# Four moves at the head of each batch of a state-space layer: dt's transfers, early scalings, MLP products, the lag of the sums

## The chip, the cores and the metric

The kernel runs on one core of a Trainium2 chip. The metric is the device time of one execution, in microseconds (us), lower being better. TensorE (PE in the rows) multiplies, PEld is its weight load, VectorE is DVE, ScalarE is ACT, GpSimd is POOL and SyncE, which issues the transfers, is SP.

## The reference, cut to what matters

Four layers run over x of 8 batches x 512 steps x 256 columns. Three are attention layers that the change doesn't touch. The fourth is a state-space layer with an MLP behind it. Its core, once forward and once on the flipped sequence, with 512 inner channels and 32 states:

```python
xdbl = x @ x_proj_W
dt = softplus(xdbl[..., :DT_RANK] @ dt_proj_W + dt_proj_b)
Bm = xdbl[..., DT_RANK:DT_RANK + D_STATE]
Cm = xdbl[..., DT_RANK + D_STATE:]
A = -exp(A_log)
def step(hst, inp):
    dt_t, B_t, C_t, x_t = inp
    dA = exp(dt_t[:, :, None] * A)
    hst = hst * dA + dt_t[:, :, None] * B_t[:, None, :] * x_t[:, :, None]
    y = einsum('bdn,bn->bd', hst, C_t)
    return (hst, y)
...
x = x + g1[:, None, :] * (fwd + bwd)
h = _ln(x, norm2_w, norm2_b)
h = h * (1.0 + s2[:, None, :]) + sh2[:, None, :]
mlp = silu(h @ w1) * (h @ w2) @ w3
return x + g2[:, None, :] * mlp
```

## The kernel before

The last layer (`mamba_layer`, L1770) takes the batches one after another. A batch is cut into 128 **units**: the forward direction is units 0 to 63, the backward one 64 to 127, and unit i handles chunk i % 4 of the channels with group i // 4 of two states (`NJ`). 128 partitions hold 64 channels x 2 states, and two such halves stand in a row of 1024. Per unit:

- ScalarE makes two decays exp(dt A) from `dt_rep` (`decay_unit`, L1957).
- dt B x: per group of four units, eight scalings (`OPS`) of `dtx_T` by a column of B give `dtx_B`. They are numbered 0 to 7. `pool_ops(k)` says how many of the last ones GpSimd makes for group k (`scale_last`, L1941); for group 0 VectorE makes the first `VEC_OPS` (`scale_first`, L1950); ScalarE makes the rest (`scale_pair`, L1933), six units ahead.
- TensorE transposes `dtx_B` into PSUM (`fill_bx`, L1967), eight transposes, called a fill here. Fill i+1 waits for scan i-1.
- VectorE scans (L2546): h = decay h + dtx_B over 1024 elements. Scan i needs fill i, its decays, and the product of unit i-3, since `h` has three slots.
- GpSimd multiplies h by C (L2512, "product with C"), into one of seven slots `hc_of`. Four of them are a tensor `hc` of their own, which lies where `dt_all` lay, three lie in slots of x.
- TensorE sums that over the states (`y_sum`, L2634), some units behind: `BEHIND` units, one fewer for each eight units from `CATCH_UP` on, never under two. Batch 0 keeps two throughout.

Between two batches come the gates, the convolution, projections and softplus of the next batch. `between_sync` sends dt out into `dt_rep`: a transfer for each of four chunks, two halves and two states, 16 in all, each with both directions (L1981). After them `sync_batch` sends C, row pair by row pair for each group (`c_rep`, four slots, L2472). At group 3 it waits for GpSimd's two additions of the MLP's result (`mlp_add`, L2505), stores the batch before, loads a new x, and only then sends C for that group.

The MLP of batch b-1 runs beside the first scans of batch b. `tanh_up` on ScalarE (L2283), a pair of products on VectorE (`mlp_products`, L2191 and L2194), three times in all (j = 0, 1, 2); the up-projections (`up_half`, L2390) and the down-projection (`down`, L2395) on TensorE, by unit in `mlp_step`; the residual (L2562) on VectorE, twice; the additions on GpSimd at units 8 and 9. The order on each engine is written out by hand: `if i in (1, 3)` puts a pair of products behind scans 1 and 3. The first fill's waits are in `first_fill`.

The first batch (0) is prepared while the layer before is running, and a barrier of all engines stands between its preparation and its first scan.

## Time and profile before

| | |
|---|---|
| median of 3 runs | 5861.52 us (5860.26 to 5861.61) |
| the profiled execution | 5858.16 us, span 5856.3 us, granted TensorE clock 0.986 |
| last layer's scans | from 3112.7 to the end of the span, 8 batches of some 346 us |
| busy over the span | PE 94%, DVE 75%, ACT 69%, POOL 48% |

The span is the time from the first to the last instruction of the profiled execution. Starts in the rows are us from the span's start. "Idle before" is the time that the engine stood before an instruction, and behind the arrow is what ended it. The granted clock is a share of TensorE's full 2.4 GHz; 0.5 is 1.2 GHz.

### The profile page before, as it was taken

How to read it: one execution, taken by the hardware profiler on the slowest of the kernel's cores; microseconds unless marked ns; L12 is line 12 of the kernel's file. 1: busy time of each engine (PE TensorE's matmuls, PEld its weight loads, DVE VectorE, ACT ScalarE, POOL GpSimd, SP SyncE). 2: the span in 40 equal slices, each digit the busy share in tenths (PEclk: the TensorE clock that was granted, in tenths of full speed). 3: DMA queues.
4: the chain of work that ended last, by engine and by line, in shares of the span. 5: the costliest groups of instructions: out<-in, count | busy, mean ns of one | idle time of the engine just before them, and what ended most of it. 6: DMA issues, size and time to landing. Idle time of an engine off the chain costs nothing. (4 is left out here: it accounts for less than half of the span.)

```text
span 5856.3 us, 74768 instructions
## 1 busy us (share of the span) xinstructions
PE 5526.3 (94%) x27336; PEld 2880.5 (49%) x27336; DVE 4380.6 (75%) x5135; ACT 4059.9 (69%) x6684; POOL 2809.0 (48%) x2191
## 2 busy tenths in 40 slices
PE   8999999999999997999998999999998999999998
PEld 5444445555555554444444444454544444454545
DVE  6767744444444445776768989999998999989998
ACT  3555454454445553555548979899898989979897
POOL 0000012232222320010107969699696979959697
PEclk8999999999999998999999999999999999999999
DMA  5242410000000004233223020110212111020110
GB/s 145 47 66 33 87 26 2 1 3 3 2 3 1 3 8 58 55 59 70 51 48 75 30 57 30 46 40 24 63 31 55 32 36 51 26 61 30 46 37 22
DMA packets 173663, 228.63 MB, mean 39 GB/s; under 512 B 41073, under 2 KB 107466, under 8 KB 173042
## 3 DMA queue, kind: packets, MB, share of 16 engines
q1 hardware_dynamic: 173298, 223.85, 17.4%
q8 instruction: 218, 3.57, 0.3%
q14 instruction: 147, 1.20, 0.1%
HBM read 156.05 MB, written 33.64 MB: 32 GB/s over the span
## 5 line engine op out<-in xcount | busy, mean ns | idle before, releaser
L2546 DVE TENSOR_TENSOR_SCAN l__h<-l__decay,psum 128x1024 f32<-128x1024 f32 x1024 | 2253.5, 2268 | 81.9 <-PE psum L1967 30.8
L1957 ACT ACTIVATE l__decay<-l__dt_rep,l__a_neg 128x511 f32<-128x511 f32 x2048 | 1342.9, 709 | 84.1 <-DVE l__h L2546 46.8
L1967 PEld LDWEIGHTS psum<-ident,l__dtx_B 128*128 128x128 f32 x8192 | 892.2, 142 | 938.0 <-DVE l__h L2546 578.4
L1967 PE MATMUL psum<-ident,l__dtx_B 128*128 128x128 f32 x8192 | 1126.1, 281 | 116.3 <-DVE l__h L2546 51.3
L2512 POOL TENSOR_TENSOR l__hc<-l__h,l__c_rep 128x1024 f32<-128x1024 f32 x584 | 1170.3, 2039 | 96.5 <-DMA l__c_rep<-l__c_dram 90.8
L1933 ACT ACTIVATE l__dtx_B<-l__dtx_T,l__b_T 128x512 f32<-128x512 f32 x1624 | 1079.5, 710 | 28.8 <-PE psum L1967 22.6
L2512 POOL TENSOR_TENSOR x_sb<-l__h,l__c_rep 128x1024 f32<-128x1024 f32 x432 | 867.1, 2040 | 32.4 <-DVE l__h L2546 20.4
L684 DVE TENSOR_REDUCE l__row_max<-psum 128x1 f32<-128x512 f32 x1024 | 648.6, 680 | 206.0 <-PE psum L718 202.3
L1373 POOL TENSOR_SCALAR l__probs<-l__probs,l__rec 128x512 f32<-128x512 f32 x512 | 349.8, 698 | 888.3 <-DVE l__rec L1369 888.3
L200 POOL TENSOR_SCALAR l__ln_var_eps<-l__ln_mean_var 128x4 f32<-128x4 f32 x56 | 16.1, 288 | 1428.5 <-DVE l__ln_mean_var L186 1428.5
L2634 PE MATMUL psum<-l__hc,l__gather 128*64 128x512 f32 x2368 | 637.2, 618 | 36.9 <-POOL l__hc L2512 36.2
L1046 ACT ACTIVATE l__probs<-psum 128x1024 f32<-128x1024 f32 x512 | 502.1, 1024 | 145.9 <-PE psum L1107 139.5
L1359 DVE TENSOR_REDUCE l__neg_max<-psum 128x2 f32<-128x1024 f32 x256 | 301.8, 1218 | 319.6 <-PE psum L1353 319.6
L2634 PE MATMUL psum<-x_sb,l__gather 128*64 128x512 f32 x1728 | 464.1, 617 | 27.4 <-POOL x_sb L2512 27.2
L1534 ACT ACTIVATE l__probs_T<-psum 128x512 f32<-128x512 f32 x256 | 152.3, 595 | 402.8 <-PE psum L1584 401.4
L718 PE MATMUL psum<-l__k_stack,l__q_stack 96*128 96x512 bf16 (+1 forms) x1024 | 380.1, 392 | 28.5 <-DVE l__row_max L684 13.9
L1941 POOL TENSOR_SCALAR l__dtx_B<-l__dtx_T,l__b_T 128x512 f32<-128x512 f32 x384 | 280.1, 729 | 155.3 <-ACT l__dtx_T L2243 154.6
L1364 ACT ACTIVATE l__probs<-psum,l__neg_max 128x512 f32<-128x512 f32 x512 | 347.3, 690 | 6.2 <-DVE l__neg_max L1359 6.1
L1107 PE MATMUL psum<-l__q_stack,l__k_stack 98*128 98x512 bf16 (+1 forms) x1024 | 302.8, 385 | 23.4 <-DMA l__q_stack<-l__max_rows 16.1
L1584 PEld LDWEIGHTS psum<-ident,l__probs 128*128 128x128 f32 x2048 | 227.6, 141 | 167.1 <-issue 98.5
L1584 PE MATMUL psum<-ident,l__probs 128*128 128x128 f32 x2048 | 278.5, 278 | 9.7 <-DVE l__probs_T L1481 7.3
L1120 PE MATMUL psum<-l__probs,l__v_and_ones 128*32 128x512 f32 x2048 | 274.3, 608 | 9.6 <-ACT l__probs L1046 9.6
(190 smaller groups left out, 6727.9 us busy)
## 6 DMA issues: line engine op xcount, KB each, us to landing
l__c_rep<-l__c_dram SPq DMA_DIRECT2D x512, 128.0 KB, 2.8
l__dt_rep<-l__dt SPq DMA_DIRECT2D x128, 256.0 KB, 5.0
l__parts_dram<-l__parts SPq DMA_DIRECT2D x64, 384.0 KB, 3.4
l__q_stack<-l__parts_dram SPq DMA_DIRECT2D x192, 128.0 KB, 6.6
l__k_stack<-l__parts_dram SPq DMA_DIRECT2D x192, 128.0 KB, 9.4
l__w<-in_l_w SPq DMA_DIRECT2D x6, 1024.0 KB, 7.6
l__gate_rows<-l__gates_dram SPq DMA_DIRECT2D x24, 256.0 KB, 3.3
in_mod_w<-in_mod_w SPq DMA_DIRECT2D x1, 4608.0 KB, 17.6
```

What stands on the lines that cost most here:

```text
L684: nc.vector.tensor_reduce(mx[:, n // GT, n % GT:n % GT + 1], max_bank(n), AX.X, ALU.max).then_inc(S["max_taken"], 1)
L718: nc.tensor.matmul(max_bank(n), qs[0:k_max, h, t * P:(t + 1) * P], ks[0:k_max, h, :], start=True, stop=True).then_inc(S["max_filled"], 1)
L1046: nc.scalar.activation(probs[:, n % SLOTS:n % SLOTS + 2, :], pair(n), ACT.Exp, scale=float(HD) ** -0.5).then_inc(S["exp"], 1)
L1364: nc.scalar.activation(probs[:, u % SLOTS, j, :], bank[QK + 2 * (u % 2) + j], ACT.Exp, bias=neg_max[:, u % SLOTS, j:j + 1], accum_out=sums ...
L1373: nc.gpsimd.tensor_scalar(probs[:, u % SLOTS, j, :], probs[:, u % SLOTS, j, :], rec[:, u % SLOTS, j:j + 1], 1.0, ALU.mult, ALU.mult)\
L1584: last = nc.tensor.transpose(bank[TR + j][:, k * P:(k + 1) * P], probs[:, u % SLOTS, j, k * P:(k + 1) * P], ident[:, :])
L1933: nc.scalar.activation(dtx_B[:, (k + 1) % 2, t, :, j, :], dtx_T[:, w, t, :].rearrange("p (b d) -> p b d", d=HB), ACT.Copy, scale=b_T[:, w, ...
L1957: nc.scalar.activation(decay[:, i % DECAYS, s, 1:T], dt_rep[:, w, c, s, 1:T], ACT.Exp, scale=a_neg[:, g, c, s:s + 1]).then_inc(S["decay"], 1)
L1967: last = nc.tensor.transpose(bx_psum(i)[:, s, t * P:(t + 1) * P], dtx_B[:, (k + 1) % 2, t, 2 * c + s, :, :].rearrange("p j d -> p (j d)"), ...
L2512: nc.gpsimd.tensor_tensor(hc_of(i), h[:, i % HS, :, :], c_of(i), ALU.mult).then_inc(S["hc"], 1)
L2546: nc.vector.tensor_tensor_scan(both(h[:, i % HS, :, :]), both(decay[:, i % DECAYS, :, :]), both(bx_psum(i)), 0.0, ALU.mult, ALU.add).then_ ...
L2634: last = nc.tensor.matmul(y_psum[half(s), c, :], gather[:, :], row, start=(w == 0 and g == 0), stop=(w == 1 and g == GROUPS - 1))
```

## The change

- `between_sync` sends the forward half of dt alone, 16 transfers of 128 KB. A new `back_sync` sends the backward half in 16 more, behind C's transfers for group 0. GpSimd waits for all of dt at unit 3, not at unit 0; ScalarE waits for the backward half at unit 64.
- The order of the seven slots is turned: the first three products go into slots of x, which dt's transfers don't read, and the wait for spilled batches moves with them from unit 4 to unit 0 of batch 0.
- Scalings: VectorE makes three of group 0 and not five, ScalarE three and not two, GpSimd two and not one. Of group 1 GpSimd makes four and not two, and all before the scans. In a batch GpSimd has 51 and not 48, 45 and not 47 of them between its products.
- The MLP's pairs of products stand behind scans 0, 1 and 4, not before scan 0 and behind 1 and 3. `tanh_up(0)` goes behind group 0's scalings and decay 1. The three down-projection steps go one unit later each. The first residual stands behind scan 6, not 5.
- `CATCH_UP` is 80, not 40.

```diff
-    pool_ops = lambda k: 1 + k % 2
-    VEC_OPS = 5
+    pool_ops = lambda k: {0: 2, 1: 4}.get(k, 1 + k % 2)
+    VEC_OPS = 3
...
-    RESIDUAL_AFTER, ADD_AT, STORE_AT, ROWS_FIRST_AT = (5, 7), (8, 9), 3, 10
-    BEHIND, CATCH_UP = 7, 40
+    PRODUCTS_AFTER, RESIDUAL_AFTER, ADD_AT, STORE_AT, ROWS_FIRST_AT = (0, 1, 4), (6, 7), (8, 9), 3, 10
+    BEHIND, CATCH_UP = 7, 80
...
-            if n < HCS - 3:
-                return hc_first[:, n, :, :]
-            return x[:, KEPT + n - (HCS - 3), :, :].rearrange("p (s u) d -> p s (u d)", s=2)
+            if n >= 3:
+                return hc_rest[:, n - 3, :, :]
+            return x[:, KEPT + n, :, :].rearrange("p (s u) d -> p s (u d)", s=2)
...
-                        sp.dma_start(dt_rep[half(j), :, c, s, :], dt_all[half(s), c, :, :]).then_inc(s_dt_rep[c], 16)
+                        sp.dma_start(dt_rep[half(j), 0, c, s, :], dt_all[half(s), c, 0, :]).then_inc(s_dt_rep[c], 16)
             sp.wait_ge(*S.at("c_out", 32))
+
+        def back_sync(sp):
+            for c in range(IC):
+                for s in range(2):
+                    for j in range(NJ):
+                        sp.dma_start(dt_rep[half(j), 1, c, s, :], dt_all[half(s), c, 1, :]).then_inc(s_dt_back, 16)
...
-                scale_last(0, range(NJ - pool_ops(0), NJ))
+                scale_last(0, range(OPS - pool_ops(0), OPS))
+                scale_last(1, range(OPS - pool_ops(1), OPS))
...
             scale_first(dve)
-            if end:
-                mlp_products(dve, 0, 0)
...
             first_decay(act, 0, nxt)
             take_forward(2)
             take_forward(3)
-            if end:
-                tanh_up(act, 0, 0)
...
             for i in range(1, DECAYED):
                 first_decay(act, i, nxt)
+            if end:
+                tanh_up(act, 0, 0)
...
+                if k == 0:
+                    back_sync(sp)
...
-                if i == 0:
+                if i == 3:
                     for c in range(IC):
                         pool.wait_ge(s_dt_rep[c], dt_rep_of(b))
+                    pool.wait_ge(s_dt_back, dt_back_of(b))
...
-                if i in (1, 3) and S.batch:
-                    mlp_products(dve, (i + 1) // 2, HC)
+                if i in PRODUCTS_AFTER and S.batch:
+                    mlp_products(dve, PRODUCTS_AFTER.index(i), HC)
```

The order of VectorE's instructions at the start of batch 1, before. `l__h` is the scan, `l__dtx_B` the early scalings, `x_sb<-x_sb,psum` the MLP's products, `x_sb<-psum,l__gate_rows` a residual:

```order
L1950 TENSOR_SCALAR l__dtx_B<-l__dtx_T,l__b_T 128x8x64 x5
L2191 SCALAR_TENSOR_TENSOR x_sb<-x_sb,psum 128x512
L2194 SCALAR_TENSOR_TENSOR x_sb<-x_sb,psum 128x512
L2546 SCALAR_TENSOR_TENSOR l__h<-l__decay,psum 128x1024 x2
L2191 SCALAR_TENSOR_TENSOR x_sb<-x_sb,psum 128x512
L2194 SCALAR_TENSOR_TENSOR x_sb<-x_sb,psum 128x512
L2546 SCALAR_TENSOR_TENSOR l__h<-l__decay,psum 128x1024 x2
L2191 SCALAR_TENSOR_TENSOR x_sb<-x_sb,psum 128x512
L2194 SCALAR_TENSOR_TENSOR x_sb<-x_sb,psum 128x512
L2546 SCALAR_TENSOR_TENSOR l__h<-l__decay,psum 128x1024 x2
L2562 TENSOR_TENSOR x_sb<-psum,l__gate_rows 128x512
```

The same place on VectorE with the change:

```order
L1953 TENSOR_SCALAR l__dtx_B<-l__dtx_T,l__b_T 128x8x64 x3
L2556 SCALAR_TENSOR_TENSOR l__h<-l__decay,psum 128x1024
L2199 SCALAR_TENSOR_TENSOR x_sb<-x_sb,psum 128x512
L2202 SCALAR_TENSOR_TENSOR x_sb<-x_sb,psum 128x512
L2556 SCALAR_TENSOR_TENSOR l__h<-l__decay,psum 128x1024
L2199 SCALAR_TENSOR_TENSOR x_sb<-x_sb,psum 128x512
L2202 SCALAR_TENSOR_TENSOR x_sb<-x_sb,psum 128x512
L2556 SCALAR_TENSOR_TENSOR l__h<-l__decay,psum 128x1024 x3
L2199 SCALAR_TENSOR_TENSOR x_sb<-x_sb,psum 128x512
L2202 SCALAR_TENSOR_TENSOR x_sb<-x_sb,psum 128x512
L2556 SCALAR_TENSOR_TENSOR l__h<-l__decay,psum 128x1024 x2
L2571 TENSOR_TENSOR x_sb<-psum,l__gate_rows 128x512
```

Two scalings are gone, scan 0 stands ahead of the first products, and three scans stand between the second and the third pair.

The order on GpSimd from the last preparation of batch 1 on, before (`l__dtx_B` is a scaling, `l__h,l__c_rep` a product with C, into `hc` or a slot of x):

```order
L2104 MEMSET l__decay 128x6
L1941 TENSOR_SCALAR l__dtx_B<-l__dtx_T,l__b_T 128x8x64
L2512 TENSOR_TENSOR l__hc<-l__h,l__c_rep 128x1024
L1941 TENSOR_SCALAR l__dtx_B<-l__dtx_T,l__b_T 128x8x64
L2512 TENSOR_TENSOR l__hc<-l__h,l__c_rep 128x1024
L1941 TENSOR_SCALAR l__dtx_B<-l__dtx_T,l__b_T 128x8x64
L2512 TENSOR_TENSOR l__hc<-l__h,l__c_rep 128x1024 x2
```

The same place with the change:

```order
L2113 MEMSET l__decay 128x6
L1944 TENSOR_SCALAR l__dtx_B<-l__dtx_T,l__b_T 128x8x64 x6
L2522 TENSOR_TENSOR x_sb<-l__h,l__c_rep 128x1024 x3
L2522 TENSOR_TENSOR l__hc<-l__h,l__c_rep 128x1024
L1944 TENSOR_SCALAR l__dtx_B<-l__dtx_T,l__b_T 128x8x64
```

Six scalings come ahead of the first product, and none stands between the first four.

The order of SyncE's transfers from batch 0 to batch 1, before:

```order
L1976 DMA l__c_dram<-l__dt_and_c 32x512 x2
L1981 DMA l__dt_rep<-l__dt 64x2x512 x16
L2472 DMA l__c_rep<-l__c_dram 64x512 x6
L2833 DMA out_x<-x_sb 128x4x256
```

And with the change:

```order
L1979 DMA l__c_dram<-l__dt_and_c 32x512 x2
L1984 DMA l__dt_rep<-l__dt 64x512 x16
L2480 DMA l__c_rep<-l__c_dram 64x512 x2
L1991 DMA l__dt_rep<-l__dt 64x512 x16
L2480 DMA l__c_rep<-l__c_dram 64x512 x4
L2844 DMA out_x<-x_sb 128x4x256
```

C's first pair now stands behind 16 transfers of half the size, and 16 more stand ahead of its second pair.

## Rows read from the trace of the kernel before

**Rows 1.** Groups of the page: op, out<-in, count | busy us, mean ns | idle before

```profile
L2546 DVE TENSOR_TENSOR_SCAN l__h<-l__decay,psum 128x1024 f32<-128x1024 f32 x1024 | 2253.5, 2268 | 81.9 <-PE psum L1967 30.8
...
L2512 POOL TENSOR_TENSOR l__hc<-l__h,l__c_rep 128x1024 f32<-128x1024 f32 x584 | 1170.3, 2039 | 96.5 <-DMA l__c_rep<-l__c_dram 90.8
```

**Rows 2.** GpSimd's busy time by stretch of batch 1: stretch, us, busy (count), clock

```profile
3446.90:3482.30 35.40, 23.73 (x16) 0.90 0.25 61
...
3500.00:3745.70 245.70, 244.80 (x157) 1.00 0.08 28
```

**Rows 3.** The chain of waits, start of batch 1: start, us, what

```profile
3450.49 4.24 DMA l__c_rep<-l__c_dram
...
3454.80 2.00 POOL l__hc L2512
...
3460.21 1.94 PE psum L1967 x8
3462.16 3.41 PE psum L2395 x8
...
3466.66 2.16 PE psum L2395 x10
```

**Rows 4.** Timeline of GpSimd, batch 1, and in the last row batch 7

```profile
3474.34 2.01 POOL L2512 TENSOR_TENSOR l__hc<-l__h,l__c_rep 128x1024 f32<-128x1024 f32 x1 [0.24 <-PE psum L2634]
...
3482.34 3.96 POOL L2512 TENSOR_TENSOR l__hc<-l__h,l__c_rep 128x1024 f32<-128x1024 f32 x2
...
3491.08 3.96 POOL L2512 TENSOR_TENSOR x_sb<-l__h,l__c_rep 128x1024 f32<-128x1024 f32 x2 [2.15 <-DMA l__c_rep<-l__c_dram]
...
5560.92 3.96 POOL L2512 TENSOR_TENSOR l__hc<-l__h,l__c_rep 128x1024 f32<-128x1024 f32 x2
```

**Rows 5.** Timeline of VectorE, batch 1, and in the last row batch 7

```profile
3446.89 4.46 DVE L2546 TENSOR_TENSOR_SCAN l__h<-l__decay,psum 128x1024 f32<-128x1024 f32 x2
...
3453.19 0.69 DVE L2194 SCALAR_TENSOR_TENSOR x_sb<-x_sb,psum 128x512 f32<-128x512 f32 x1
...
3468.90 0.67 DVE L2562 TENSOR_TENSOR x_sb<-psum,l__gate_rows 128x512 f32<-128x512 f32 x1
...
3474.69 2.28 DVE L2546 TENSOR_TENSOR_SCAN l__h<-l__decay,psum 128x1024 f32<-128x1024 f32 x1
...
5525.26 4.46 DVE L2546 TENSOR_TENSOR_SCAN l__h<-l__decay,psum 128x1024 f32<-128x1024 f32 x2
```

**Rows 6.** Timeline of the sync queue's transfers into batch 1: start, us of issuing, count

```profile
3433.43 15.73 SPq L1981 DMA_DIRECT2D l__dt_rep<-l__dt  x16
3449.26 9.89 SPq L2472 DMA_DIRECT2D l__c_rep<-l__c_dram  x6
```

**Rows 7.** All engines by stretch: us, PE, PEld, DVE, ACT, POOL, clock, DMA, GB/s

```profile
3440.00:3450.00 10.00, 8.69 (x43) 5.14 (x42) 7.97 (x11) 8.39 (x14) 0.70 (x1) 1.00 1.06 237
...
3454.00:3459.00 5.00, 0.63 (x2) 0.00 (x0) 4.14 (x2) 5.00 (x9) 4.20 (x3) 1.00 0.15 52
3459.00:3466.00 7.00, 5.79 (x20) 4.99 (x21) 3.77 (x4) 5.56 (x10) 7.00 (x6) 0.51 0.11 40
```

**Rows 8.** Timeline of ScalarE, batch 1

```profile
3453.91 2.56 ACT L1957 ACTIVATE l__decay<-l__dt_rep,l__a_neg 128x511 f32<-128x511 f32 x4 [1.48 <-DMA l__dt_rep<-l__dt]
```

**Rows 9.** Who writes `dtx_B`, ns min/median/max: VectorE in batch 1, GpSimd in batch 3

```profile
L1950 DVE TENSOR_SCALAR l__dtx_B<-l__dtx_T,l__b_T x5: 467/473/789, 3443.1 to 3445.0; 128x512 f32<-128x512 f32 x5
...
L1941 POOL TENSOR_SCALAR l__dtx_B<-l__dtx_T,l__b_T x1: 994/994/994, 4137.2 to 4137.2; 128x512 f32<-128x512 f32 x1
```

**Rows 10.** Timeline of TensorE, batches 1 and 3

```profile
3495.56 1.09 PE L1967 MATMUL psum<-ident,l__dtx_B 128*128 128x128 f32 x8 [2.22 <-DVE l__h L2546]
...
4137.06 2.58 PE L2390 MATMUL psum<-x_sb,l__w 128*128 128x512 f32 x4 [1.93 <-ACT l__dtx_T L2243]
...
4145.18 1.88 PE L2390 MATMUL psum<-x_sb,l__w 128*128 128x512 f32 x4
```

**Rows 11.** Timeline of GpSimd, batch 0

```profile
3127.22 3.98 POOL L2512 TENSOR_TENSOR x_sb<-l__h,l__c_rep 128x1024 f32<-128x1024 f32 x2
```

More of the change, by code:

```diff
@@ L1787, in mamba_layer @@
     ADDED_AT = tuple(range(4 * IC, 8 * IC, IC))
-    pool_ops = lambda k: 1 + k % 2
-    VEC_OPS = 5
-    scaled = lambda groups: sum(OPS - pool_ops(k % GROUPS) for k in range(1, groups + 1)) \
+    pool_ops = lambda k: {0: 2, 1: 4}.get(k, 1 + k % 2)
+    VEC_OPS = 3
+    scaled = lambda groups: sum(OPS - pool_ops(k % (2 * GROUPS)) for k in range(1, groups + 1)) \
         - (VEC_OPS if groups == UNITS // IC else 0)
-    pool_scaled = lambda groups: sum(pool_ops(k % GROUPS) for k in range(1, groups + 1))
-    RESIDUAL_AFTER, ADD_AT, STORE_AT, ROWS_FIRST_AT = (5, 7), (8, 9), 3, 10
-    BEHIND, CATCH_UP = 7, 40
+    pool_scaled = lambda groups: sum(pool_ops(k) for k in range(2, min(groups + 1, 2 * GROUPS))) \
+        + (pool_ops(0) + pool_ops(1) if groups == UNITS // IC else 0)
+    PRODUCTS_AFTER, RESIDUAL_AFTER, ADD_AT, STORE_AT, ROWS_FIRST_AT = (0, 1, 4), (6, 7), (8, 9), 3, 10
+    BEHIND, CATCH_UP = 7, 80
     FILLED = 2
@@ L1852, in mamba_layer @@
         dt_rep_of = lambda b: PER_CHUNK * (b + 1)
+        s_dt_back = nc.alloc_semaphore(f"{tag}_dt_back")
+        dt_back_of = lambda b: PER_CHUNK * IC * (b + 1)
         psum = consts["psum"]
@@ L1928, in scale_pair @@
             w, g, _ = split(k * IC)
-            for op in (2 * c, 2 * c + 1)[0:NJ - pool_ops(k) if c == IC - 1 else NJ]:
-                if k == 0 and op < VEC_OPS:
+            for op in (2 * c, 2 * c + 1):
+                if op >= OPS - pool_ops(k) or k == 0 and op < VEC_OPS:
                     continue
@@ L1938, in scale_last @@
             w, g, _ = split(k * IC)
-            t = TT - 1
-            for j in ops:
+            for op in ops:
+                t, j = op // NJ, op % NJ
                 nc.gpsimd.tensor_scalar(dtx_B[:, (k + 1) % 2, t, :, j, :],
@@ L2346, in first_fill @@
                 pe.wait_ge(*S.at("dtxB", scaled(UNITS // IC) if end else OPS - pool_ops(0) - VEC_OPS))
-                pe.wait_ge(*S.at("dtxB_pool", pool_scaled(UNITS // IC) if end else pool_ops(0)))
+                pe.wait_ge(*S.at("dtxB_pool", pool_scaled(UNITS // IC) - pool_ops(1) if end else pool_ops(0)))
                 pe.wait_ge(*S.at("dtxB_vec", VEC_OPS))
@@ L2408, in mlp_step @@
                         down(pe, t, j)
-            if i == 4:
+            if i == 5:
                 pe.wait_ge(*S.at("prod", 0))
@@ L2415, in mlp_step @@
                 down(pe, 2, 2)
-            if i == 5:
+            if i == 6:
                 for j in range(HC):
@@ L2489, in gpsimd_batch @@
                 k = i // IC + 1
-                if i % IC == (1 if k == 1 else 0) and k < UNITS // IC:
-                    if k >= 2:
-                        pool.wait_ge(*S.at("bx_filled", IC * (k - 1) - FILLED))
-                    scale_last(k, (NJ - pool_ops(k),))
-                if i % IC == (2 if k == 1 else 1) and k < UNITS // IC and pool_ops(k) == 2:
-                    scale_last(k, (NJ - 1,))
+                if i % IC == 0 and 2 <= k < UNITS // IC:
+                    pool.wait_ge(*S.at("bx_filled", IC * (k - 1) - FILLED))
+                    scale_last(k, (OPS - pool_ops(k),))
+                if i % IC == 1 and 2 <= k < UNITS // IC and pool_ops(k) == 2:
+                    scale_last(k, (OPS - 1,))
                 if i % IC == 0:
                     pool.wait_ge(*S.at("c_rep", 16 * NJ * (i // IC + 1)))
-                if i == 0:
+                if i == 3:
                     for c in range(IC):
                         pool.wait_ge(s_dt_rep[c], dt_rep_of(b))
+                    pool.wait_ge(s_dt_back, dt_back_of(b))
                 if i in ADD_AT and S.batch:
@@ L2506, in gpsimd_batch @@
                     pool.wait_ge(*S.at("mlp_add", k - 1))
-                if i == HCS - 3 and b == 0:
+                if i == 0 and b == 0:
                     pool.wait_ge(s_spill, 16 * (B - KEPT))
@@ L2593, in decays @@
                     act.wait_ge(s_dt_rep[i], dt_rep_of(b))
+                if i == UNITS // 2:
+                    act.wait_ge(s_dt_back, dt_back_of(b))
                 decay_unit(i)
@@ L2598, in scalar_batch @@
             for i in range(UNITS):
-                if i in (1, 3) and S.batch:
-                    tanh_up(act, (i + 1) // 2, HC)
+                if i in PRODUCTS_AFTER[1:] and S.batch:
+                    tanh_up(act, PRODUCTS_AFTER.index(i), HC)
                 if i + DECAYED < UNITS:
```

5 lines of the change are left out of this document (2 added, 3 removed).

## The prediction

> **What bounds the kernel now.** The change touches the last layer alone, so I read in this order: the costliest groups, GpSimd's time by stretch, the chain of waits at the start of a batch, and the timelines of GpSimd and VectorE there.
>
> In the groups the reader should see two operations of nearly the same size per unit: the scan on VectorE and the product with C on GpSimd, both some 2.0 to 2.3 us [rows 1]. GpSimd also has 1.5 scalings for every 4 units. In batch 1 GpSimd is busy 244.8 us of the 245.7 us from unit 16 or so to unit 126, so it sets the pace there; in the 35.4 us before, it works 23.7 us [rows 2]. What can be won lies in those first 35 us, and a gain there is kept only if it reaches GpSimd.
>
> The chain of waits says what fills them [rows 3]. It comes down the sync queue's sixteen dt transfers, through C's first transfer (lands 3454.7), the first product with C (3454.8), a scaling behind it, and then TensorE at half clock: 8 transposes in 1.94 us, 8 matmuls of the MLP in 3.41 us. That first product starts 7.9 us after scan 0, and the tenth, unit 9, at 3482.34 [rows 4], 35.45 us after scan 0 [rows 5]. In the last batch, 7, that distance is 35.66 us, and over the seven batches with an MLP beside the scans, read from the same rows of each, it is 34.9 in the mean [rows 4, 5]. I use it as the yardstick, and call the start of scan 0 time 0.
>
> **The transfers.** Before, sixteen dt transfers of 256 KB take the sync queue 15.73 us, and C's follow at 3449.26, or +2.4 [rows 6]. The DMA engines are full at 237 GB/s meanwhile [rows 7], so 256 KB need 1.1 us and the issue time (0.98 us) is their backlog. Sixteen of 128 KB should take 0.6 us each: they begin at -13.5 as before and end at -3.9. C's first pair goes out by -2.6 and, with the 4.24 us of [rows 3], lands by +1.6, ahead of scan 0's end at +2.2. The sixteen backward ones follow from -2.6 to +7 and land by about +10; C's second pair lands by +11.5. Unit 3's product, which now waits for all dt, cannot begin before +11.7, and unit 4's, which needs C's second pair, not before +14.4. So they cost nothing, with 1.7 us to spare at the tighter place. ScalarE's waits for dt, the longest 1.48 us [rows 8], go.
>
> **The first fill.** VectorE's five early scalings take 2.4 us (last start 3445.0, first 3443.1, and 0.47); the first took 0.79 us instead of 0.47 beside GpSimd's one, and where VectorE began first GpSimd's took 0.99, 0.3 us over its usual time [rows 9]. They get in each other's way by about 0.3 us. Now VectorE has three and GpSimd runs six beside them: three of 0.41 us plus three meetings of 0.3 to 0.4 us make 2.2 to 2.4 us. Bounds: with no further meeting the fill comes 0.43 us sooner, which is how long TensorE idled before it; if every one costs a whole slot, 0.2 us later. I take 0, because the meeting is in the rows. The Trainium skill (SBUF — State Buffer, "SBUF: two separate sides") says that the port pair shared by VectorE's two-port mode and GpSimd is an exclusive lock for a whole instruction, which speaks against giving GpSimd more scalings here. By that rule the seven starts lose 1.4 us together; without it they gain 3.0 us; the traces fit the lock. ScalarE has three scalings (2.0 us) and GpSimd's first two are done in time. Its four for the second group end at about +0.5, under the wait for scan 0. No such scaling is left between the first products, so TensorE's fill 4 no longer waits for one.
>
> **VectorE from scan 0 to scan 8.** A scan takes a 2.2 us slot, a pair of MLP products 1.4, a residual 0.7 [rows 5]. In the new order: scan 0 ends 2.2, products 3.6, scan 1 5.8, products 7.2, scans 2 to 4 13.9, products 15.3, scans 5 and 6 19.7, residual 20.4, scan 7 22.6, residual 23.2, where scan 8 starts. It is 8 x 2.2 + 3 x 1.4 + 2 x 0.7 = 23.2 us of plain work; before, batch 1 took 27.8 us although one pair was done ahead of scan 0 [rows 5]. Who must be ready:
> - ScalarE: three scalings, decay 1, tanh 0 by -0.1, four scalings 2.4, decay 2 3.7, tanh 1 4.3 (needed 5.8). Ready.
> - TensorE at full clock, a fill 1.09 and an up-projection 1.88 us [rows 10]: fill 2 ends 3.8 (needed 7.2), fill 3 7.0 (9.4), fill 4 10.6 (11.7), fill 5 12.8 (15.3), eight down matmuls at 0.22 us each (from ten in 2.16 us [rows 3]) 14.7, fill 6 15.8 (17.5), ten more 18.1, fill 7 19.2 (20.4). Ready each time.
> - GpSimd: products 0 to 3 start at 2.3, 5.9, 9.5, 11.7; scan 5 needs product 2, ended 11.5, and scan 6 product 3, ended 13.7. Ready.
>
> **The sum.** Product 7 starts after scan 7 and the first sum, at 22.9. From there to product 9 GpSimd has the same work as before, 3474.34 to 3482.34, 8.0 us [rows 4]. Product 9 thus starts at 30.9 against 34.9: 4.05 us won, seven times, 28.4 us. From there on nothing changes: the wait of 2.15 us before unit 12 [rows 4] is for C's fourth pair, behind the store that GpSimd's second addition releases, and it moves along.
>
> Batch 0 has no MLP and starts behind a barrier that waits for the queue's issues. Product 4 starts at 3127.22 [rows 11]. The barrier opens about 1 us sooner, but now product 3 waits for the backward dt (some 3123) and C's second pair comes after it (some 3125.5): I take 1.1 us won, bounds 0 and 3.
>
> The longer lag of the sums (7 up to unit 80) costs nothing: units up to 40 have had it, and GpSimd still idles under 1 us in 245 [rows 2]. Without that cover each product would wait for its slot as unit 7 does, 0.24 us [rows 4].
>
> Sum: 28.4 + 0 + 1.1 = 29.5 us. The profiled execution took 5858.2 us, so 5828.7 in its terms. The median of the runs is 3.4 us above it, 5861.5, and my forecast is on that: 5832 us, 0.50% less.
>
> **The rivals.**
> - *TensorE falls to half clock again.* It does so soon after pauses of 1.93 and 2.22 us [rows 10]; my order leaves it 0.7 and 1.1 us near +9 to +12, shorter, but close together. At half clock the eight down matmuls take 3.4 instead of 1.75 us and a fill 1.94, which makes scan 7 late by 1.3 to 2.1 us: 9 to 15 us over seven batches, 5841 to 5847. Against it: the 5 us with 0.63 us of TensorE work that came before a granted clock of 0.51 in 3459 to 3466 [rows 7] are gone. Chance 0.16.
> - *Slower: a transfer costs the queue the same whatever its size.* If 128 KB take 1.0 us each as 256 KB do, C's first pair lands at +7.9 as before, the backward sixteen are issued until +20 and land by +25. Product 3 begins then instead of at +15.2, product 4 at +27.7, product 9 at about +41.5: 6.6 us lost seven times, and some 10 in batch 0, 5918. For it: C's own first 128 KB took 1.19 us. Against: that was behind the backlog, and six C transfers together span 9.89 us with their landings waited for in between [rows 6]. It starts to cost when a backward transfer takes over 0.9 us (14.3 us from -2.6 to +11.7, by sixteen). Chance 0.05.
> - *The gain is swallowed at unit 12.* If C's fourth pair came at a fixed time and not 8.7 us after GpSimd's additions, six of the seven gains would end in that wait: 5857. The queue's store follows the addition at once in batch 1, so little speaks for it. Chance 0.05.
>
> **Numbers.** My forecast has 0.74, in a range of its own from 5822 to 5840 (no meeting on the port -3, batch 0 -2, a batch's late half-clock stretch behind unit 12 up to 1 us in four batches, and up to 1 us a batch that my hand-made order has missed). This kernel's measurement can tell some 0.2%, 12 us, from no change. The range for 8 in 10 takes in the clock case: 5818 to 5850. Faster by over 0.2% (below 5849.8): 0.74 and nearly all of 0.16, 0.88. Within 0.2%: 0.07. Slower: 0.05.
>
> **What would show it.** Right: product 0 within 0.2 us of scan 0's end in batches 1 to 7; scan 8 at 23 to 24 us after scan 0; product 9 at about 31; granted clock 1.00 in the first 20 us; no wait for dt on ScalarE or GpSimd; three VectorE scalings that take 2.2 us or more together, and scan 0 within 0.3 us of where it was behind the scan before it. Wrong: TensorE rows of 0.45 us there (first rival), product 3 or 4 released by a transfer in batches 1 to 7 (second), a wait before unit 12 of 6 us in place of 2 (third). If scan 8 comes at 23 and product 9 later than 32, GpSimd's path has something that I have not seen.

## The result and the profile after

The changed kernel took **5822.99 us** (median of 4 runs, 5820.22 to 5827.71) against 5860.89 (5858.82 to 5861.61) for the kernel before on the same chip: ratio 0.9937, 95% interval 0.9921 to 0.9952. A second set on another chip gave 5824.93 us and 0.994 [0.9926, 0.9953]. The forecast was 5832 us, in 5818 to 5850. The profiled executions, which I compare below, took 5820.22 us (span 5818.4, granted clock 0.989) after and 5858.16 before, 37.9 us apart, where the sum said 29.5.

The groups, in the same columns as [rows 1], show the same two operations at nearly the same size. The first three products of a batch now stand in slots of x, so both of GpSimd's groups have to be read: together they idled 128.9 us before, 102.8 of them for C's transfers, and idle 77.5 now, 21.0 of them for C. The largest releaser is now the scan.

```profile
L2556 DVE TENSOR_TENSOR_SCAN l__h<-l__decay,psum 128x1024 f32<-128x1024 f32 x1024 | 2252.3, 2267 | 60.9 <-POOL l__hc L2522 20.6
...
L2522 POOL TENSOR_TENSOR l__hc<-l__h,l__c_rep 128x1024 f32<-128x1024 f32 x576 | 1145.1, 2010 | 27.0 <-DVE l__h L2556 13.2
...
L2522 POOL TENSOR_TENSOR x_sb<-l__h,l__c_rep 128x1024 f32<-128x1024 f32 x440 | 876.1, 2010 | 50.5 <-DVE l__h L2556 40.1
```

The sync queue's timeline into batch 1 answers to [rows 6]. Sixteen transfers of 128 KB take 10.10 us to issue, C's first pair goes at 3442.36, and the backward sixteen take as long again. The second-last row is the store of the previous batch, the last C behind it.

```profile
3432.17 10.10 SPq L1984 DMA_DIRECT2D l__dt_rep<-l__dt  x16
3442.36 1.18 SPq L2480 DMA_DIRECT2D l__c_rep<-l__c_dram  x2
3443.58 10.37 SPq L1991 DMA_DIRECT2D l__dt_rep<-l__dt  x16
3454.00 5.32 SPq L2480 DMA_DIRECT2D l__c_rep<-l__c_dram  x4
3475.80 0.41 SPq L2844 DMA_DIRECT2D out_x<-x_sb  x1
...
3479.76 15.79 SPq L2480 DMA_DIRECT2D l__c_rep<-l__c_dram  x10
```

VectorE's timeline of batch 1 answers to [rows 5]. Scan 0 starts at 3445.60, scan 8 at 3468.18, 22.58 us later, with no idle time in between. Behind the three early scalings (2.35 us) it idles 1.41 us for the first fill.

```profile
3441.85 2.35 DVE L1953 TENSOR_SCALAR l__dtx_B<-l__dtx_T,l__b_T 128x512 f32<-128x512 f32 x3
3445.60 2.29 DVE L2556 TENSOR_TENSOR_SCAN l__h<-l__decay,psum 128x1024 f32<-128x1024 f32 x1 [1.41 <-issue]
3447.80 0.66 DVE L2199 SCALAR_TENSOR_TENSOR x_sb<-x_sb,psum 128x512 f32<-128x512 f32 x1
...
3449.10 2.28 DVE L2556 TENSOR_TENSOR_SCAN l__h<-l__decay,psum 128x1024 f32<-128x1024 f32 x1
...
3467.60 0.67 DVE L2571 TENSOR_TENSOR x_sb<-psum,l__gate_rows 128x512 f32<-128x512 f32 x1
3468.18 4.45 DVE L2556 TENSOR_TENSOR_SCAN l__h<-l__decay,psum 128x1024 f32<-128x1024 f32 x2
```

GpSimd's timeline of the same stretch answers to [rows 4]. Each of the first products waits for its scan, not for a transfer. Product 9 starts at 3475.80, 30.20 us after scan 0. The wait before unit 12 is still there, 1.95 us against 2.15.

```profile
3441.56 4.52 POOL L1944 TENSOR_SCALAR l__dtx_B<-l__dtx_T,l__b_T 128x512 f32<-128x512 f32 x6 [15.04 <-ACT l__dtx_T L2251]
3448.04 2.00 POOL L2522 TENSOR_TENSOR x_sb<-l__h,l__c_rep 128x1024 f32<-128x1024 f32 x1 [1.96 <-DVE l__h L2556]
3451.46 2.00 POOL L2522 TENSOR_TENSOR x_sb<-l__h,l__c_rep 128x1024 f32<-128x1024 f32 x1 [1.42 <-DVE l__h L2556]
...
3467.83 2.00 POOL L2522 TENSOR_TENSOR x_sb<-l__h,l__c_rep 128x1024 f32<-128x1024 f32 x1 [0.84 <-DVE l__h L2556]
...
3475.80 2.00 POOL L2522 TENSOR_TENSOR x_sb<-l__h,l__c_rep 128x1024 f32<-128x1024 f32 x1
...
3484.34 3.96 POOL L2522 TENSOR_TENSOR l__hc<-l__h,l__c_rep 128x1024 f32<-128x1024 f32 x2 [1.95 <-DMA l__c_rep<-l__c_dram]
```

All engines by stretch, in the columns of [rows 7]: the hole of 5 us in which TensorE worked 0.63 us is a stretch with 3.20 us of work, and the granted clock behind it is 1.00 where it was 0.51.

```profile
3454.00:3459.00 5.00, 3.20 (x22) 2.65 (x22) 5.00 (x3) 4.09 (x7) 3.78 (x2) 1.00 0.47 108
3459.00:3466.00 7.00, 7.00 (x45) 5.99 (x43) 6.96 (x7) 6.47 (x12) 5.87 (x5) 1.00 0.10 37
```

Read from the start rows of scans and products in each batch, means of batches 1 to 7 in us:

| | before | after | difference, seven batches |
|---|---|---|---|
| last scan of a batch to scan 0 | 49.89 | 49.49 | 2.8 |
| scan 0 to product 0 | 7.89 | 2.44 | |
| scan 0 to scan 8 | 27.28 | 22.58 | |
| scan 0 to product 9 | 34.92 | 30.21 | 33.0 |
| product 9 to the last scan | 260.97 | 260.86 | 0.8 |

That is 36.6 us. Batch 0 gave nothing, and the layer's first softplus came 1.3 us sooner (3092.67 against 3094.00): 37.9. I take the last as chance and not as an effect of the change: in the profiles of this study that softplus starts anywhere from 3092.7 to 3102.7 us (3097.95 in a second profile of the changed kernel, e12), though no edit here touches what runs ahead of it. So I judge an edit by its distances inside the batches first and by the ratio second.

### The profile page after: what moved, and what is told of

The parts are those of the page before. It is cut to its first block and busy times, and to the rows that moved or that the text cites. A ratio compares the mean times of both kernels' runs of the same rounds, so it can differ in the third digit from the quotient of the medians.

```text
span 5818.4 us, 74898 instructions
## 1 busy us (share of the span) xinstructions
PE 5519.2 (95%) x27336; PEld 2866.2 (49%) x27336; DVE 4375.3 (75%) x5119; ACT 4054.8 (70%) x6676; POOL 2826.3 (49%) x2215
## 5 line engine op out<-in xcount | busy, mean ns | idle before, releaser
L2522 POOL TENSOR_TENSOR l__hc<-l__h,l__c_rep 128x1024 f32<-128x1024 f32 x576 | 1145.1, 2010 | 27.0 <-DVE l__h L2556 13.2
L2645 PE MATMUL psum<-l__hc,l__gather 128*64 128x512 f32 x2304 | 618.3, 618 | 12.0 <-POOL l__hc L2522 12.0
L2645 PE MATMUL psum<-x_sb,l__gather 128*64 128x512 f32 x1792 | 483.2, 619 | 12.8 <-POOL x_sb L2522 12.3
```

What stands on the lines that cost most here:

```text
L2522: nc.gpsimd.tensor_tensor(hc_of(i), h[:, i % HS, :, :], c_of(i), ALU.mult).then_inc(S["hc"], 1)
L2645: last = nc.tensor.matmul(y_psum[half(s), c, :], gather[:, :], row, start=(w == 0 and g == 0), stop=(w == 1 and g == GROUPS - 1))
```

## The experiments

Each starts from the changed kernel. They ask which of the four moves brought the 33 us, why it was more than the sum said, and whether the costs I saw (the meeting of VectorE's and GpSimd's scalings, unit 12) are what I took them for. Where two medians of different experiments are compared, their ratios to the kernel before on the same chip say more than the microseconds.

### e1: dt sent whole again

```diff
-    sp.dma_start(dt_rep[half(j), 0, c, s, :], dt_all[half(s), c, 0, :]).then_inc(s_dt_rep[c], 16)
+    sp.dma_start(dt_rep[half(j), :, c, s, :], dt_all[half(s), c, :, :]).then_inc(s_dt_rep[c], 16)
...
-    if k == 0:
-        back_sync(sp)
```

(The two waits for the backward half go as well.)

> The changed kernel, but with dt's forward and backward halves sent together again in sixteen transfers, ahead of C's. C's first pair then lands at about +7.9 us after scan 0, as before the change, not at +2.4. My theory: with no scaling between the first products and VectorE's work spread out, that costs little. Product 0 at 7.9, product 1 at 9.9, scan 3 starts at 9.9 in place of 9.2, scan 4 at 12.1; product 9 at 31 to 31.5 us and not 30.2. 0.8 to 1.3 us a batch, 6 to 9 us over seven, and 2.4 us more if one batch's decay 0 waits for dt as batch 3's did: 5829 to 5834 us. Rival: C's first transfer is on the path all the way, as the chain of waits of the kernel before has it. Then the 5.5 us by which it lands later show in full at product 9, seven times: some 5860 us.

Measured: 5833.97 us (5831.4 to 5837.19), ratio 0.9956 [0.9941, 0.9971], at the upper end of what was expected. Product 0 at 8.0, scan 8 at 23.96, product 9 at 32.26 us, 0.8 later than expected. The sixteen transfers take 15.87 us again. TensorE's timeline of batch 1 shows the half clock that the prediction had as a rival: a pause of 1.80 us, a fill in 1.97 us instead of 1.06, eight down matmuls in 2.63 instead of 1.89. The down matmuls then push the first sum to 3468.65, and the last row, GpSimd's, shows product 7 waiting for it.

```profile
3455.39 1.06 PE L1970 MATMUL psum<-ident,l__dtx_B 128*128 128x128 f32 x8 [0.78 <-DVE l__h L2553]
3458.26 1.97 PE L1970 MATMUL psum<-ident,l__dtx_B 128*128 128x128 f32 x8 [1.80 <-DVE l__h L2553]
3460.02 2.63 PE L2403 MATMUL psum<-l__w,x_sb 128*128 128x256 f32 x8
...
3468.65 1.08 PE L2640 MATMUL psum<-x_sb,l__gather 128*64 128x512 f32 x4
```

```profile
3469.82 2.00 POOL L2519 TENSOR_TENSOR x_sb<-l__h,l__c_rep 128x1024 f32<-128x1024 f32 x1 [1.61 <-PE psum L2640]
```

The split is worth 2.05 us a batch up to product 9 and 0.33 between batches, over half of the latter in batch 3 (1.26 of 2.3). That is 16.7 of the 36.6 us, not all of it: something else in the change must bring the rest even with C late.

### e2: the scalings in their old places

```diff
-    pool_ops = lambda k: {0: 2, 1: 4}.get(k, 1 + k % 2)
-    VEC_OPS = 3
+    pool_ops = lambda k: 1 + k % 2
+    VEC_OPS = 5
...
-                scale_last(1, range(OPS - pool_ops(1), OPS))
```

> The changed kernel with the scalings as before: five on VectorE, one on GpSimd ahead of the scans, two of group 1 between the first products. My theory: with C landing early, GpSimd has 1.42 and 1.49 us idle ahead of products 1 and 2, which take in the two scalings of 0.66 us; the last one ends by +8.5, fill 4 starts at +11.1. VectorE's five alone take what three took beside six of GpSimd's (2.36 and 2.35 us). So product 9 stays at 30.2 us, gap between batches as it is, 5823 us within 4. Rival: the two scalings more in GpSimd's stretch cost their 1.3 us a batch, product 9 at 31.5, 5832 us.

Measured: 5821.61 us (5816.07 to 5832.45), ratio 0.9931 [0.9915, 0.9948]; product 9 at 30.22 and the gap before scan 0 49.43 us, against 30.21 and 49.49. With C early the moved scalings are worth nothing, because GpSimd idles before each of its first three products anyway (1.96, 1.42 and 1.49 us in batch 1 of the changed kernel): in e2 its two scalings of group 1 are done 8.54 us after scan 0, and fill 4, which needs them, starts at 9.43 in both kernels.

### e3: the MLP's products in their old places

```diff
-    PRODUCTS_AFTER, RESIDUAL_AFTER, ADD_AT, STORE_AT, ROWS_FIRST_AT = (0, 1, 4), (6, 7), (8, 9), 3, 10
+    PRODUCTS_AFTER, RESIDUAL_AFTER, ADD_AT, STORE_AT, ROWS_FIRST_AT = (0, 1, 3), (5, 7), (8, 9), 3, 10
...
             scale_first(dve)
+            if end:
+                mlp_products(dve, 0, 0)
...
-                if i in PRODUCTS_AFTER and S.batch:
+                if i in PRODUCTS_AFTER[1:] and S.batch:
```

(tanh 0 goes back ahead of ScalarE's scalings, and each group of down matmuls goes one unit earlier, as before.)

> The changed kernel with the MLP's order as before: first pair of products and tanh 0 ahead of scan 0, pairs behind scans 1 and 3, down steps and first residual one unit earlier. My theory: in the changed kernel VectorE idles 1.41 us ahead of scan 0, so the first pair is free there and costs 1.3 us behind scan 0. Undone, with dt and C early enough, VectorE's plain work from scan 0 to scan 8 falls from 22.6 to 21.2 us and all that it waits for is ready: product 9 at 29 us, 1.0 to 1.3 us a batch faster, 5814 to 5816 us. Rival: the move was what took ScalarE's tanh and TensorE's down steps off the path (1.1 us wait for tanh, 1.7 to 2.2 us before scans 4 and 5 in the kernel before), so that undoing it gives back 1 to 3 us a batch: 5830 to 5844 us.

Measured: 5814.48 us (5810.77 to 5817.78), ratio 0.9922 [0.9907, 0.9937], the gap unchanged at 49.49 us, scan 8 at 21.27 and product 9 at 28.88. **The MLP move costs 1.33 us a batch, 9.3 in all.** VectorE idles 1.41 us for the first fill; a pair of products takes 1.3 us and fits in there, as its timeline in this kernel shows:

```profile
3443.41 2.34 DVE L1953 TENSOR_SCALAR l__dtx_B<-l__dtx_T,l__b_T 128x512 f32<-128x512 f32 x3
3445.67 0.67 DVE L2201 SCALAR_TENSOR_TENSOR x_sb<-x_sb,psum 128x512 f32<-128x512 f32 x1
3446.37 0.69 DVE L2204 SCALAR_TENSOR_TENSOR x_sb<-x_sb,psum 128x512 f32<-128x512 f32 x1
3447.16 4.46 DVE L2558 TENSOR_TENSOR_SCAN l__h<-l__decay,psum 128x1024 f32<-128x1024 f32 x2
```

The change takes the pair out of that hole and puts it behind scan 0, where VectorE is the bound: here it is busy 28.81 of the 28.88 us from scan 0 to product 9 (stretch, us, busy and count, clock, share and rate of the DMA).

```profile
3447.16:3476.04 28.88, 28.81 (x18) 1.00 0.36 87
```

### e4: the longer lag of the sums alone undone

```diff
-    BEHIND, CATCH_UP = 7, 80
+    BEHIND, CATCH_UP = 7, 40
```

> The changed kernel with CATCH_UP 40 in place of 80. My theory: GpSimd sets the pace from unit 16 on and the sums wait for nobody: the same time within 2 us, and from unit 40 to 80 the same distance. Rival: sums that run closer behind the products make TensorE wait for GpSimd and delay its fills: up to 0.24 us a unit in units 40 to 80, which would be over 5 us a batch.

Measured: 5823.94 us (5820.12 to 5830.79), ratio 0.994 [0.9925, 0.9955]. Units 40 to 80 take 90.29 us, and 90.31 with the longer lag. It does nothing.

### e8 and e10: one move alone, and two without the split

e8 keeps the split and undoes scalings and MLP order, the diffs of e2 and e3 together.

> The changed kernel with both the scalings and the MLP's order as before: of the change only the split of dt, the turned slots and the lag are left. My theory: what the two undone parts were worth each by itself (nothing, and a loss of 1.32 us a batch) adds up, as GpSimd has idle time for the scalings there too: product 9 at 28.9 us, 5814 us within 4. Rival: with VectorE 1.3 us further ahead, the scalings between the first products now hold up fill 4 or GpSimd: product 9 at 29.5 to 30.2, 5819 to 5823 us.

Measured: 5819.48 us (5815.93 to 5821.0), ratio 0.9923 [0.9909, 0.9936]; product 9 at 28.91, gap 49.44 us. The split alone keeps all that e3 has inside the head of a batch. The time is 1.5 us above the band expected and inside the rival's, but the rival's product 9 (29.5 or later) didn't come, and the ratio is e3's (0.9922) within the noise.

e10 undoes split and MLP order, the diffs of e1 and e3.

> The changed kernel with dt whole again and the MLP's order as before: only the scalings, the slots and the lag are new. Before all that product 9 was at 34.9 us in the mean; with dt whole and the MLP's order new it is at 32.3. My theory: with C's first pair landing at +7.9 GpSimd works without a pause from there, and 22.4 us more bring it to product 9 at 30.4 at best; what is over that is TensorE's half clock. The scalings out from between the first products are what brought 34.9 down, not the MLP's order: product 9 at 31 to 33 us, 5828 to 5838 us, as with the new order. Rival: the MLP's order did it: product 9 stays at 34 to 35 us and the time at 5850 us or more.

Measured: 5835.31 us (5827.23 to 5839.98), ratio 0.9949 [0.9936, 0.9963]; product 9 at 31.19, gap 49.95 us. So the scalings alone, beside a dt sent whole, bring product 9 from 34.92 to 31.19, although e2 had found them worthless. The last corner was needed. Product 0 starts at 7.92 us here, as late as before.

### e11: neither split nor scalings, only the MLP order and the lag

The diffs of e1 and e2 together.

> Scalings in their old places and dt sent whole; only the MLP slots and the sums' lag are those of the change. Theory (the six scalings and the split both remove the same wait, GpSimd's late start for want of dt, so either alone brings most of it): without either, product 9 goes back to 35 to 36.5 us after scan 0, scan 8 to 27 to 28.5, gap 49.9; the time is 5860 to 5872 us, ratio 1.000 to 1.002. Rival (the scalings are worth nothing, as with the split present, and what the kernel with dt whole gained over the kernel before came from the later MLP slots): product 9 at 32 to 32.5 us, 5829 to 5838 us, ratio 0.995 to 0.9965.

Measured: 5858.62 us (median of 10 runs, 5846.9 to 5868.39), ratio 0.9993 [0.9984, 1.0002]; product 9 at 34.22, scan 8 at 26.38, gap 49.92 us. The rival, 32 to 32.5 us, falls, and with neither of the two the gain is gone. But the theory's numbers were all too late (product 9 at 35 or more, scan 8 at 27 or more, 5860 us or more), and it named the wrong wait. It blamed GpSimd's late start, and product 0 is as late in e10 and e1 (7.92 and 8.02 us), where most of the gain is there. What is gone in those two is TensorE's wait before fill 4. In the kernel before, that fill waited for a scaling of GpSimd's:

```profile
3460.21 1.94 PE L1967 MATMUL psum<-ident,l__dtx_B 128*128 128x128 f32 x8 [5.58 <-POOL l__dtx_B L1941]
```

In e11 TensorE's row names ScalarE instead:

```profile
3462.41 3.33 PE L1969 MATMUL psum<-ident,l__dtx_B 128*128 128x128 f32 x16 [4.69 <-ACT l__dtx_B L1935]
```

The name misleads. Fill 4 needs the eight scalings of group 1, and in the old table six of them are ScalarE's and two GpSimd's. Behind the two of group 0 at 3445.05, ScalarE's six are the four and two of these rows, the last done at 3454.14, 8.3 us before the fill. The one that ended at 3462.31 belongs to group 2; it counts up the same semaphore.

```profile
3448.82 2.55 ACT L1935 ACTIVATE l__dtx_B<-l__dtx_T,l__b_T 128x512 f32<-128x512 f32 x4
...
3452.82 1.32 ACT L1935 ACTIVATE l__dtx_B<-l__dtx_T,l__b_T 128x512 f32<-128x512 f32 x2
```

GpSimd's two stand behind products 0 and 1, and product 0 waits 11.21 us for C. The second is done at 3462.30, and the fill starts 0.1 us later:

```profile
3457.00 2.00 POOL L2518 TENSOR_TENSOR x_sb<-l__h,l__c_rep 128x1024 f32<-128x1024 f32 x1 [11.21 <-DMA l__c_rep<-l__c_dram]
3458.98 0.69 POOL L1943 TENSOR_SCALAR l__dtx_B<-l__dtx_T,l__b_T 128x512 f32<-128x512 f32 x1
...
3461.61 0.69 POOL L1943 TENSOR_SCALAR l__dtx_B<-l__dtx_T,l__b_T 128x512 f32<-128x512 f32 x1
```

In all seven batches of both kernels fill 4 starts 0.1 us behind that scaling, in the mean 13.30 us after scan 0 before and 13.31 in e11. The new table lets GpSimd make its share of group 1, four and not two, before scan 0, while it has nothing else to do; fill 4 then starts at 9.45 us (e1) and 8.20 (e10) in the mean, though C is late. With the split C is early, the two products are done early, and the scalings between them too.

Product 9 in us after scan 0, means of batches 1 to 7, for the eight combinations:

| | dt whole | dt split |
|---|---|---|
| old scalings, old MLP order | 34.92 (before) | 28.91 (e8) |
| old scalings, new MLP order | 34.22 (e11) | 30.22 (e2) |
| new scalings, old MLP order | 31.19 (e10) | 28.88 (e3) |
| new scalings, new MLP order | 32.26 (e1) | 30.21 (after) |

Split and scalings remove the same wait: fill 4 behind GpSimd's scaling behind C. Beside the old MLP order the split alone is worth 6.0 us a batch and the scalings alone 3.7; with the split the scalings add 0.03. The MLP order costs 1.1 to 1.3 us wherever that wait is gone. Where both keep it, it seems to gain 0.7: fill 5 follows fill 4 at once in e11, where the kernel before puts eight down matmuls (3.62 us) between them. That one difference is not clean, since the first cell is the kernel before itself, which also lacks the turned slots, the longer lag and the later wait for dt. Only the lag was tried apart (e4).

### e5: GpSimd's four scalings of group 1 held back

```diff
+                pool.wait_ge(*S.at("dtxB_vec", VEC_OPS))
                 scale_last(1, range(OPS - pool_ops(1), OPS))
```

> The changed kernel, but GpSimd begins its four early scalings of group 1 only when VectorE's three of group 0 are done. In the changed kernel VectorE's three take 2.35 us (0.69, 0.91 and 0.91 us) and TensorE idles 0.41 us for the last of them. My theory: they alternate with GpSimd's for the port, one for one; with only two of GpSimd's beside them the third meeting goes, the fill starts 0.4 us sooner, and the gap between the last scan of a batch and scan 0 of the next falls from 49.49 to 49.1 us in each of seven batches: 3 us in all, 5820 us, with product 9 where it was. Rival: something else holds the fill at that place (ScalarE's third scaling, which ends 0.7 us before VectorE's, or TensorE's up-projection): the gap stays at 49.49.

Measured: the gap falls from 49.49 to 49.05 us in all seven batches, as expected. In the timeline VectorE's three scalings take 1.91 us instead of 2.35, and GpSimd's last four, which now wait for them, 2.69.

```profile
3456.11 1.91 DVE L1953 TENSOR_SCALAR l__dtx_B<-l__dtx_T,l__b_T 128x512 f32<-128x512 f32 x3
```

```profile
3458.11 2.69 POOL L1944 TENSOR_SCALAR l__dtx_B<-l__dtx_T,l__b_T 128x512 f32<-128x512 f32 x4 [0.77 <-DVE l__dtx_B L1953]
```

The time doesn't show it: 5827.91 us (5824.43 to 5831.17), ratio 0.9939 [0.9926, 0.9951], where I had expected 5820. In this profile two things cost more than the 3.1 us won: the layer began 5.0 us later than in the profile of the changed kernel, and batch 0 waited 8.06 us before product 16 instead of 0.41. The second goes with the split and varies: it is 0.41 to 8.06 us in the nine profiles of kernels that have the split (2.98 in e9, with e5's wait in it, and 0.87 in e12, the changed kernel again), and nothing in the kernel before, e1 and e11 (0.81 in e10). Why it is longest here stays open.

```profile
3165.00 2.00 POOL L2523 TENSOR_TENSOR x_sb<-l__h,l__c_rep 128x1024 f32<-128x1024 f32 x1 [8.06 <-DMA l__c_rep<-l__c_dram]
```

### e6: the store one group of C later

```diff
-    PRODUCTS_AFTER, RESIDUAL_AFTER, ADD_AT, STORE_AT, ROWS_FIRST_AT = (0, 1, 4), (6, 7), (8, 9), 3, 10
+    PRODUCTS_AFTER, RESIDUAL_AFTER, ADD_AT, STORE_AT, ROWS_FIRST_AT = (0, 1, 4), (6, 7), (8, 9), 4, 10
```

> The changed kernel with STORE_AT 4 in place of 3: C's fourth pair goes out ahead of the wait for GpSimd's additions, and the store, the load of x and the gate rows go between the fourth and the fifth. My theory: the wait before unit 12 (1.6 to 3.1 us in batches 1 to 6) is the landing of C's fourth pair some 8.6 us after the additions; it goes, and with it TensorE's half clock and the 0.92 us at units 16 and 24 in four of the batches. The fifth pair then lands by about +38 and is needed at +45. From product 9 to product 12 6.55 us in all batches in place of 8.2 to 9.7, to product 16 8.51: 12.5 and 3 us, 5807 us. Rival: the wait only moves to unit 16, since the store, the load and the gate rows are as slow there: 5820 us or more.

Measured: products 9 to 12 in 6.55 us in each of the seven batches, instead of 8.34 in the mean: the wait before unit 12 is gone. But in three of the seven batches, 1, 4 and 7, product 9 came at 31.18 us instead of 30.22. There TensorE fell to half clock, the prediction's first rival. The pauses before fills 4 and 5 are 0.78 and 1.02 us in every batch, as in the changed kernel, but fill 5 takes 1.88 us in batch 1 and 1.09 in batch 2 (third row), and the granted clock of batch 1's next 4.4 us is 0.61:

```profile
3467.92 1.88 PE L1970 MATMUL psum<-ident,l__dtx_B 128*128 128x128 f32 x8 [1.02 <-DVE l__h L2556]
3469.60 2.82 PE L2403 MATMUL psum<-l__w,x_sb 128*128 128x256 f32 x8
...
3807.61 1.09 PE L1970 MATMUL psum<-ident,l__dtx_B 128*128 128x128 f32 x8 [1.02 <-DVE l__h L2556]
```

The down matmuls and the first sum come late by it, and product 7 waits 1.80 us for that sum instead of 0.83 for its scan:

```profile
3479.60 2.00 POOL L2522 TENSOR_TENSOR x_sb<-l__h,l__c_rep 128x1024 f32<-128x1024 f32 x1 [1.80 <-PE psum L2645]
```

What makes the clock fall in these three and in none of the 35 batches of the changed kernel, e2, e4, e5 and e12, whose product 9 is at 30.19 to 30.22, this doesn't show. Product 9's mean of 30.64 us and the shorter rows behind it leave the last scan 1.7 us sooner per batch (289.33 against 291.07). The time is 5817.61 us (5813.81 to 5819.02), ratio 0.9918 [0.9903, 0.9934]; I had said 5807. The profile was at 5819.02. Beside the changed kernel's profile (5820.22) it puts 7.2 us on the layer's later start, 3.5 us on batch 0 (2.9 of them the wait before product 16, 3.28 against 0.41) and 2.9 us on the half clock in three batches. In the sync queue's timeline C's second to fourth pairs now go together, ahead of the store:

```profile
3464.86 10.00 SPq L2480 DMA_DIRECT2D l__c_rep<-l__c_dram  x6
3487.60 0.41 SPq L2844 DMA_DIRECT2D out_x<-x_sb  x1
```

### e9: the old MLP order, the later store and e5's wait together, and e12: the changed kernel beside it

The old MLP order (e3), the later store (e6) and the wait of e5, on the changed kernel. The two ran on one chip.

> The change with three pieces altered: the MLP's products in their old place (after the scaling, one behind scan 3), the store of the batch before one group of C later (STORE_AT 4), and GpSimd's four scalings of group 1 held until VectorE's three are done. If the three add, per batch: product 9 at 28.9 us after scan 0 instead of 30.2, products 9 to 12 in 6.6 us instead of 8.3, the gap before scan 0 at 49.05 us instead of 49.49, so some 3.3 to 3.5 us of each of seven batches and 23 to 25 us in all: 5796 to 5801 us where the change takes 5821 to 5824, ratio to the kernel before 0.989 to 0.9905. Rival: the later store delays the residual sums' read or the scaling of group 2 and product 9 stays at 30 us or more in some batches, as it did in three of seven with the later store alone: 5802 to 5808 us. A second rival: the earlier layers start late again and swallow it in one profile; then the distances inside the batches still read as above.

> The changed kernel itself once more, beside the others on this chip, to compare with them directly. Both theories: 5818 to 5828 us, ratio 0.993 to 0.9945; product 9 at 30.2 us after scan 0 and gap 49.5 us in every batch from 1 to 7, while the first softplus of the layer comes anywhere from 3092 to 3102 us.

Measured, e9: **5800.26 us** (5793.33 to 5804.67), ratio 0.9894 [0.988, 0.9907]. e12: 5824.93 us (5821.72 to 5829.97), ratio 0.994 [0.9926, 0.9953], gap 49.49 and product 9 at 30.21 us again, the first softplus at 3097.95. The three add: gap 49.05, product 9 at 28.94, products 9 to 12 in 6.55 us, every batch within 0.16 us of these. The rival (product 9 at 30 or more) did not come: in this order TensorE's pauses are shorter at fills 4 and 5, and its next one, 1.75 us before fill 8, is followed by a fill in 1.06 us in all seven batches. Scan 0 to the last scan takes 287.46 us against 290.68 in e12. With the gap that is 25.7 us over seven batches, and the medians are 24.7 apart. GpSimd's timeline of batch 1 shows products 12 and 13 following products 10 and 11 and a scaling without a wait:

```profile
3479.31 3.96 POOL L2525 TENSOR_TENSOR l__hc<-l__h,l__c_rep 128x1024 f32<-128x1024 f32 x2
3483.25 0.70 POOL L1944 TENSOR_SCALAR l__dtx_B<-l__dtx_T,l__b_T 128x512 f32<-128x512 f32 x1
3483.90 3.96 POOL L2525 TENSOR_TENSOR l__hc<-l__h,l__c_rep 128x1024 f32<-128x1024 f32 x2
```

## Why the prediction was right, and where its sizes were off

- **Transfers** (sixteen at 0.6 us, C by +1.6). Measured 10.10 us for sixteen, 0.63 each; product 0 starts at +2.44 behind scan 0 in batches 1 to 7. Of their products 0 to 11 one is released by a transfer: product 3 of batch 3, where the backward dt is the last to come and costs 0.28 us (the others wait 0.27 there for the scan), so the product could start 1.9 us later there than the +10 I gave for dt, and the margin of 1.7 was used up. ScalarE's waits for dt went but for two, of 0.78 us in batch 3 and 0.55 in batch 7. In the main right, and the rival of a price per transfer (5918 us) is out. GpSimd's row of that batch, with scan 0 at 4128.60:

```profile
4140.50 2.00 POOL L2522 TENSOR_TENSOR l__hc<-l__h,l__c_rep 128x1024 f32<-128x1024 f32 x1 [0.55 <-DMA l__dt_rep<-l__dt]
```

- **VectorE, scan 0 to 8** (23.2 us). Measured 22.58, always plain work, as the sum had it. The terms were rounded up: a scan's slot is 2.18 and not 2.2, a pair 1.3 and not 1.4, a residual 0.6 and not 0.7. That is 0.6 us a batch, 4.2 of the 4.6 us by which the head's gain (33.0) passed 28.4.
- **From scan 8 to product 9** (7.7 us). 7.6.
- **The first fill** (0, bounds -0.43 and +0.2 us). Measured against the kernel before: 0.08 us sooner in the six batches other than 3; against the old scalings beside the same split (e2): 0.06 us later. VectorE's three took 2.35 us, inside the forecast 2.2 to 2.4. e5 gives the size of the meeting, 0.44 us, the bound the sum had named for a kernel without one. The Trainium skill (SBUF — State Buffer, "SBUF: two separate sides") has VectorE in its two-port mode and GpSimd exclude each other for a whole instruction. The trace agrees in kind: a scaling of VectorE's beside GpSimd's took up to 0.91 us for 0.47, one of GpSimd's up to 0.86 for 0.69, and their ends alternate. By the records the block is shorter than the whole instruction, though: VectorE's second ended 0.28 us behind GpSimd's second, where one takes 0.47 alone. e5's wait brought back only part, since GpSimd's first two still meet VectorE's.
- **Between batches otherwise** (nothing). Here the sum missed a term: 2.8 us, 2.4 of them in batch 3. There ScalarE waited 3.27 us for dt before its first decay (the prediction had 1.48 us [rows 8] for its longest such wait), and TensorE then ran in part at half clock (2.58 us for four matmuls [rows 10]); I had used that batch's row for the pauses and not asked what the split does to it. After, the gap there is 49.48 us like all others.
- **Batch 0** (1.1, bounds 0 and 3). Measured 0. Scan 0 comes 1.7 us sooner behind the softplus. Product 3 begins at 3123.07 after 3.98 us of waiting and product 4 at 3125.70, against 3123 and 3125.5 forecast. But the last scan is not earlier: product 16 waits for C, and TensorE behind it. What I left out is that the weights and gates, which the sync queue sends in batch 0 between C's fourth and fifth pairs, also move back behind sixteen more transfers: C's fifth pair, which product 16 needs, lands 42.7 us after scan 0 and not 34.9. How long that stall lasts differs between runs, 0.41 us here and 8.06 in e5.
- **Lag of the sums** (0). e4: 0.02 us in 40 units.
- **Half clock** (chance 0.16). It did not come: TensorE's pauses at that place are 0.78 and 1.02 us, and the granted clock stays 1.00. The rival was a real one: in e6 it came with the same pauses in three of seven batches, and there it cost 0.96 us a batch at product 9, where the prediction had 1.3 to 2.1 at scan 7.
- **Unit 12** (chance 0.05). 1.95 us for 2.15, not 6. The wait moves along, as argued, and e6 shows that it hangs on the store.

The result lies 1 us inside the forecast's own range (5822 to 5840), and the profile's gain is 8.4 us over the sum's 29.5: 4.6 from the head, 2.8 between batches, 0.8 behind product 9 and 1.3 from the earlier start, less the 1.1 that batch 0 didn't give. The path was the one predicted, GpSimd's first products behind C and fill 4 behind GpSimd's scaling; that the total came so near is in part luck, since the earlier start is none of the change's. What the sum did not say, though it had the parts for it, is which move earns what. It counted the MLP order as three pairs and two residuals in one row of plain work, and so never asked what the first pair had cost in its old place. The pair was nearly free there, in VectorE's wait for the first fill, and moving it costs 9.3 us. The scalings I had priced at the first fill alone, right beside the split and wrong without it.
